# A vision tower with three expert layers: the last layer's blocks write the output, repeated tokens are routed once

## The reference

```python
logits = x @ router_w                       # 8 experts
probs = softmax(logits); p = max(probs); e_idx = argmax(probs)
combine = one_hot(e_idx) * p[:, None]
out = sum over e of combine[:, e] * (relu(x @ wi[e]) @ wo[e])   # 192 -> 768 -> 192
h = _layernorm(h + out)                     # this is the result
```

## Time and profile before

| | us |
|---|---|
| median of 3 runs | 2679.78 |
| lowest and highest run | 2667.89, 2680.46 |
| span of the profiled execution | 2663.7 |
| TensorE busy in it | 2220.1 (83%) |
| VectorE, ScalarE, GpSimd busy | 1463.9, 888.3, 907.3 |

### The profile page before, as it was taken

The page is one execution under the profiler, slowest core; times in us unless marked ns, Lnnn a source line. Parts: engine busy times, 40 slices in busy tenths (PEclk is TensorE's granted clock), DMA queues, the critical chain, the costliest instruction groups (busy, mean ns, idle before and its releaser), DMA issues. The chain is left out here.

```text
span 2663.7 us, 47821 instructions
## 1 busy us (share of the span) xinstructions
PE 2220.1 (83%) x18071; PEld 1965.6 (74%) x18071; DVE 1463.9 (55%) x3517; ACT 888.3 (33%) x1921; POOL 907.3 (34%) x817
## 2 busy tenths in 40 slices
PE   8999995699699749987999889998999967564792
PEld 8888883477588639985766679998999966443692
DVE  2677767566577746227999733332432236866213
ACT  0333336522254313334555411111111114764111
POOL 0323235600100253338776502301111136554325
PEclk9999986699899759998999989999999989555796
DMA  9500000160000336540000050104666631002452
GB/s 271 184 1 1 1 1 19 37 192 2 1 2 2 140 94 184 176 131 21 16 11 6 1 205 26 31 1 160 210 209 211 213 117 39 1 1 79 133 178 74
DMA packets 125725, 225.21 MB, mean 85 GB/s; under 512 B 15862, under 2 KB 96306, under 8 KB 118458
## 3 DMA queue, kind: packets, MB, share of 16 engines
q1 hardware_dynamic: 114938, 203.87, 23.3%
q0 software_dynamic: 10560, 18.29, 2.4%
HBM read 169.06 MB, written 53.02 MB: 83 GB/s over the span
## 5 line engine op out<-in xcount | busy, mean ns | idle before, releaser
L2596 POOL COPY bl_swiglu_w<-ahead_w2swiglu_w 128x1152 f32 x53 | 60.7, 1147 | 370.6 <-PE psum L2648 275.9
L2690 ACT ACTIVATE bl_swiglu_sg<-psum 128x384 f32<-128x384 f32 x106 | 52.0, 490 | 311.9 <-PE psum L2637 311.9
L2626 PE MATMUL psum<-bl_swiglu_xt,bl_swiglu_w 128*128 128x128 f32 x1272 | 152.9, 278 | 1.7 <-DVE bl_swiglu_hid L2727 1.1
L2626 PEld LDWEIGHTS psum<-bl_swiglu_xt,bl_swiglu_w 128*128 128x128 f32 x1272 | 151.0, 194 | 2.3 <-issue 2.3
L2717 DVE COPY bl_swiglu_xt<-psum 128x256 f32<-128x256 f32 x53 | 22.5, 425 | 207.1 <-PE psum L2607 207.1
L2099 POOL DMA_INDIRECT rows_in<-tower_h,tower_spots x66 | 65.3, 990 | 157.2 <-DVE tower_spots L2997 124.3
L2702 ACT ACTIVATE bl_gelu_hid<-psum,bl_gelu_w 128x128 f32<-128x128 f32 x270 | 74.2, 377 | 115.9 <-POOL bl_gelu_w L2596 112.9
L2648 PE MATMUL psum<-bl_swiglu_w,bl_swiglu_hid 128*128 128x192 f32 x636 | 112.1, 327 | 0.0
L2596 POOL COPY bl_gelu_w<-ahead_w2gelu_w 128x1350 f32 x45 | 60.3, 1362 | 149.9 <-DVE bl_gelu_y L2737 136.9
L2929 ACT ACTIVATE shared_sg<-psum 128x432 f32<-128x432 f32 x66 | 35.0, 530 | 206.5 <-PE psum L2866 206.5
L2648 PEld LDWEIGHTS psum<-bl_swiglu_w,bl_swiglu_hid 128*128 128x128 f32 x636 | 102.1, 190 | 0.1
(11 more groups left out here) (683 smaller groups left out, 6062.8 us busy)
## 6 DMA issues: line engine op xcount, KB each, us to landing
bl_swiglu_w<-in_swiglu_w SPq DMA_DIRECT2D x53, 1152.0 KB, 5.2
rows_in<-tower_zeros SPq DMA_DIRECT2D x2, 14592.0 KB, 47.8
bl_gelu_w<-in_gelu_w SPq DMA_DIRECT2D x45, 576.0 KB, 4.0
bl_relu_w<-in_relu_w SPq DMA_DIRECT2D x26, 576.0 KB, 4.1
ahead_w2swiglu_w<-in_swiglu_w SPq DMA_DIRECT2D x1, 9216.0 KB
tok_x<-in_x SPq DMA_DIRECT2D x11, 648.0 KB, 12.5
ahead_w2gelu_w<-in_gelu_w SPq DMA_DIRECT2D x1, 5400.0 KB
bl_swiglu_xr<-rows_in SPq DMA_DIRECT2D x53, 96.0 KB, 2.0
```

The source lines that it names most:

```text
L2596: pool.tensor_copy(w2[:, n % DEEP], w2all[:, e, :].rearrange("p e n -> p (e n)")).then_inc(s_w2, 1)
L2626: pe.matmul(up_tile(n, j, i, side), w[:, o:o + 128], xt[:, n % 2, side, :], start=(i == 0), stop=False, skip_group_check=True)
L2690: act.activation(sg[:, j], bank_pair(n, j)[:, 0, 0:3 * BLOCK].rearrange("p (i n) -> p i n", i=3), ACT.Silu).then_inc(s_silu, 1)
```

## The change

It does these things. (1) Repeated tokens are no longer routed: the tokens are laid so that the last tile begins with image 63 and then repeats 61 and 62, `own` gives the 36 rows of it that are sent, and `chose` is zero for the others. In the gelu and swiglu layers `find_slots` gives the repeated rows the slots of the first ones. `block_count` goes by 2304 rows. (2) In the last layer the row that is sent has two more columns, the gate and the token's row number in the output (`last_rows`, `LAST` = 194), and goes to a DRAM array of its own, `rows_last`, which `clear_last` fills with zeros during the attention stage. (3) A relu block adds its fetched rows to gate times result, takes the variance, and four blocks later scales the rows; GpSimd raises to the power and scatters them to their place in `out` by indirect DMA. Empty rows have token number 0 and go to spare rows ahead of the output. (4) `stage_output` is gone, and so are slots and stores of the last layer. Not shown: `stage_output` as removed, the passing of `cst["xs"]`, the same `choose` and `find_slots` in `stage_shared`, names of tiles and semaphores, and the quantised stage's levelling into the new rows (`rest.level(pool, t, ends[:, t, 0:D])` and the like).

```diff
-MAXB = 53
-DEPTH = (NT * T + BLOCK - 1) // BLOCK
+MAXB = 51
+TOK = 64 * IMG
+DEPTH = (TOK + BLOCK - 1) // BLOCK
 WAY = 4
 FF = 512
+LAST = D + 2
+SPARE = (TOK + (BLOCK - 1) * 8) // BLOCK * BLOCK
...
+def clear_last(sp, cst):
+    sp.dma_start(cst["xl"].rearrange("(a p) n -> p a n", p=128),
+                 cst["fill"][:].unsqueeze(1).broadcast_to([128, 8 * DEPTH + 1, LAST])).then_inc(cst["blank"], 16)
+def last_rows(cst):
+    return cst["xT"][0:T].rearrange("p a n -> p (a n)")[:, 0:NT * LAST].rearrange("p (t n) -> p t n", n=LAST)
...
-    return (NT * T * top + (BLOCK - 1) * E) // BLOCK
+def own(t):
+    return IMG if t == NT - 1 else T
+def choose(dve, chose, iota, picks, a, b, TOP, E):
+    for x, y in ((a, min(b, NT - 1)), (NT - 1, b)):
+        if x < y:
+            rows = own(x)
+            ins = dve.tensor_tensor(chose[0:rows, x:y], iota[0:rows, 0:E].unsqueeze(1).unsqueeze(1).broadcast_to([rows, y - x, TOP, E]),
+                                    picks[0:rows, x:y, :].unsqueeze(3).broadcast_to([rows, y - x, TOP, E]), ALU.is_equal)
+    return ins
+def find_slots(then, dve, cst, sl, found, TOP):
+    then(dve.tensor_tensor(found[:, :, 0:TOP], sl[:], found[:, :, 0:TOP], ALU.add))
+    then(dve.scalar_tensor_tensor(found[:, NT - 1, 0:TOP], found[:, NT - 2, 0:TOP], cst["twice"][:, 0:1], found[:, NT - 1, 0:TOP],
+                                  ALU.mult, ALU.add))
+    then(dve.tensor_copy(cst["slots"][:, 0:TOP].rearrange("p c t -> p t c"), found[:, :, 0:TOP]))
+def send_rows(pool, cst, rows, TOP, tiles, to):
     for t in tiles:
+        n = own(t)
         for c in range(TOP):
-            at = bass.IndirectOffsetOnAxis(ap=cst["spots"][:, t, c:c + 1], axis=0)
-            pool.indirect_dma_start(out=cst["xs"], out_offset=at, in_=rows[:, t, :], in_offset=None).then_inc(cst["sent"], 16)
+            at = bass.IndirectOffsetOnAxis(ap=cst["spots"][0:n, t, c:c + 1], axis=0)
+            pool.indirect_dma_start(out=to, out_offset=at, in_=rows[0:n, t, :], in_offset=None).then_inc(cst["sent"], 16)
             cst["sent_count"] += 16
...
-                    if kind != "swiglu":
-                        if gelu:
-                            pool.wait_ge(cst["clean"], 32)
-                        for g, (a, b) in enumerate(groups):
-                            pool.wait_ge(c_slot, g + 1)
-                            send_rows(pool, cst, rows, TOP, range(a, b))
+                    if gelu:
+                        pool.wait_ge(cst["clean"], 32)
+                    else:
+                        pool.wait_ge(cst["blank"], 16)
+                    for g, (a, b) in enumerate(groups):
+                        pool.wait_ge(c_slot, g + 1)
+                        send_rows(pool, cst, rows, TOP, range(a, b), cst["xs"] if gelu else cst["xl"])
                 @block.tensor
...
                         ins.then_inc(c_T, 1)
-                    act.wait_ge(c_d, 1)
+                        if not gelu and p >= 4 and p % 2 == 0:
+                            powers(act, p // 2 - 2)
                     if gelu:
+                        act.wait_ge(c_d, 1)
                         act.activation(sc[:, 1, :], sc[:, 0, :], ACT.Exp).then_inc(c_e, 1)
                     else:
-                        act.activation(lo[:], lo[:], ACT.Exp).then_inc(c_e, 1)
+                        for g in range((NP - 1) // 2 - 1, NG):
+                            powers(act, g)
                 @block.vector
...
                         a, b = groups[g]
                         n = b - a
+                        if not gelu:
+                            dve.wait_ge(c_e, g + 1)
+                            K.then(dve.tensor_reduce(sc[:, 0, a:b], lo[:, a:b, 0:E], AX, ALU.add))
+                            dve.reciprocal(rows[:, a:b, D], sc[:, 0, a:b])
                         dve.wait_ge(p_m, g + 1)
                         ranked = bank(PO[g % 2])[0:T, 0:n * E].rearrange("p (t e) -> p t e", e=E)
...
                     dve.wait_ge(laid, all_laid)
+                    dve.memset(chose[:, NT - 1], 0.0)
+                    if not gelu:
+                        dve.tensor_copy(rows[:, :, D + 1], cst["token"][:])
                     K.then(dve.tensor_copy(base[:, 0], cst["seed"][:, 0:E]))
...
             @block.sync
             def _(sp):
                 S.arrived(sp, s_w)
+                clear_last(sp, cst)
                 S.clear_before(sp)
...
+        shelves = cst["xl" if last else "xs"].rearrange("(b p) n -> b p n", p=BLOCK)
+        XR = KEPT if last else DEEP
+        WX = LAST if last else D
         w2all = cst["ahead"]["w2" + kind]
         with Stage(nc, "bl_" + kind, cst) as S:
             sg = S.sb("sg", [128, 2, 3, BLOCK])
-            y = S.sb("y", [128, 2, D])
+            y = S.sb("y", [128, KEPT if last else 2, D])
+            to = S.sb("to", [128, KEPT], mybir.dt.uint32)
+            st = S.sb("st", [128, KEPT, 6])
+            mv = S.sb("mv", [128, KEPT, 2])
...
             with nc.Block() as block:
                 @block.sync
                 def _(sp):
                     def fetch_rows(n):
-                        if n >= DEEP:
-                            sp.wait_ge(p_T, n - DEEP + 1)
-                        b = bass.ds(sp.value_load(place[0:1, n:n + 1], min_val=0, max_val=E * DEPTH - 1), 1)
-                        sp.dma_start(xr[:, n % DEEP], shelves[b].rearrange("b p n -> (b p) n")).then_inc(s_x[n % DEEP], 16)
+                        if n >= XR:
+                            sp.wait_ge(c_y if last else p_T, n - XR + 1)
+                        b = bass.ds(sp.value_load(place[0:1, n:n + 1], min_val=0, max_val=E * DEPTH - (not last)), 1)
...
                             store(n - 3)
-                    for n in range(NB if glu else NB - 3, NB):
+                    for n in range(NB if glu or last else NB - 3, NB):
                         store(n)
-                    for x in range(2):
-                        sp.wait_ge(s_st[x], 16 * ((NB + 1 - x) // 2))
+                    ways = len(s_st)
+                    for x in range(ways):
...
                 def _(pool):
+                    def power(n):
+                        x = n % KEPT
+                        pool.wait_ge(c_var, n + 1)
+                        pool.tensor_tensor(rt[:, x:x + 1], vt[:, x:x + 1], cst["half"][:, 0:1], ALU.pow).then_inc(g_root, 1)
+                    def scatter(n):
+                        x = n % KEPT
+                        pool.wait_ge(c_z, n + 1)
+                        pool.indirect_dma_start(out=cst["out"], out_offset=bass.IndirectOffsetOnAxis(ap=to[:, x:x + 1], axis=0),
+                                                in_=y[:, x, :], in_offset=None).then_inc(s_st[x], 16)
                     pool.wait_ge(s_all, 1)
                     for n in range(NB):
                         e = bass.ds(pool.value_load(owner[0:1, n:n + 1], min_val=0, max_val=E - 1), 1)
                         if n >= DEEP:
                             pool.wait_ge(c_y if kind == "gelu" else s_dn, n - DEEP + 1)
                         pool.tensor_copy(w2[:, n % DEEP], w2all[:, e, :].rearrange("p e n -> p (e n)")).then_inc(s_w2, 1)
+                        if last and n >= 4:
+                            power(n - 4)
+                        if last and n >= 6:
+                            scatter(n - 6)
+                    if last:
+                        for n in range(NB - 6, NB):
+                            if n + 2 < NB:
+                                power(n + 2)
+                            scatter(n)
                 @block.tensor
                 def _(pe):
                     def turn(n):
-                        pe.wait_ge(s_x[n % DEEP], arrivals(n))
+                        pe.wait_ge(s_x[n % XR], arrivals(n, XR))
                         if n >= 2:
                             pe.wait_ge(c_T, n - 1 if glu else n - n % 2)
-                        x = xr[:, n % DEEP]
+                        x = xr[:, n % XR]
                         pe.transpose(tp[:, n % 2, 0:BLOCK], x[:, 0:128], ident[:])
                         pe.transpose(tp[:, n % 2, BLOCK:2 * BLOCK], x[:, 64:192], ident[:]).then_inc(p_T, 1)
...
                             dve.wait_ge(s_w2, n + 1)
+                        if last:
+                            x = n % KEPT
+                            if n >= KEPT:
+                                dve.wait_ge(s_st[x], 16 * (n // KEPT))
+                            dve.tensor_tensor(to[:, x:x + 1], xr[:, n % XR, D + 1:D + 2], cst["spare"][:, n:n + 1], ALU.max)
+                            dve.scalar_tensor_tensor(y[:, x], dn[:, n % 2, 0:D], xr[:, n % XR, D:D + 1], xr[:, n % XR, 0:D],
+                                                     ALU.mult, ALU.add).then_inc(c_y, 1)
+                            dve.wait_ge(c_y, n + 1)
+                            K.then(dve.bn_stats(st[:, x, :], y[:, x]))
+                            K.then(dve.bn_aggr(mv[:, x, :], st[:, x, :]))
```

(36 more changed lines are left out.)

125 lines of the change are left out of this document (45 added, 80 removed).

## The result

| | before | after |
|---|---|---|
| median of the runs in one comparison | 2676.70 us (2667.89 to 2680.46, 4 runs) | 2608.73 us (2604.46 to 2612.17, 4 runs) |
| span of the profiled execution | 2663.7 us | 2602.6 us |
| ratio | | 0.9751, 95% interval 0.9730 to 0.9772 |

2614.7 us had been forecast, in a range of 2600 to 2631. The profiled execution has a span of 2602.6 and a time of 2604.46, so 1.9 us lie around the span; in the later runs it was 1.8 to 2.0.

A forecast was written before the change was run, and what follows sets the result against it. TensorE was taken to bound the block stages, GpSimd's chain of gathers the 48.7 us last stretch. Terms -13.1 - 8.7 - 43.6 + 0.7 - 0.4 = -65.1 gave a span of 2598.6, with 16.1 carried 2614.7 us, range 2600 to 2631.

The forecast's parts named there:

- Swiglu blocks: Swiglu layer: block count falls from 53 to 51, two blocks of 6.54 us saved, -13.1 us.
- Gelu pair: Gelu layer: block count falls from 45 to 43, so one whole pair goes, -8.7 us.
- batch statistics: Batch statistics drop two calls shorter than the 0.36 us of a full one, on the path: -0.4 us.
- Relu blocks' steady part: Relu pairs stay 8.72 us; added VectorE work hidden, 2.4 us cover left. T is when a pair of down-products ends.
- The tail: After the last full relu pair ends (T), three scatters follow one another; end at T+13.2, -43.6 us, one block included.
- The relu route: Last layer's routing: gate exponentials and sums move into the loop over six groups, +0.7 us, bounds -0.4 and +3.
- The fill: New 14.4 MB fill at the start of the attention stage is hidden, 0; 48 us if not hidden.
- The time carried: Whole kernel: the median before lies 16.1 us above the profiled span; that distance was added to the forecast span.
- 1 (VectorE the bound): Relu blocks: VectorE operations held for a weight copy's length leave 1.0 us uncovered per pair, 12 us, 2627; chance 0.12.
- 2 (a worse tail): Tail and relu route: late power, slow scatter landings or slips in every group, together +8 us, 2623; chance 0.12.
- 3 (the fill collides): The new fill collides with the loads or the mapping of queues after it: +48 us, 2663; chance 0.02.
- 4 (GpSimd the clock): Relu blocks: GpSimd's queue decides the pair from a scatter of 2.4 us; slower than before, 2692 at 5.5; chance 0.01.

The follow-up runs named there:

- before_again: The kernel before, run once more unchanged: 2671.44 us, one run.
- store_only: The kernel after with the leaving out of repeated tokens undone, so only the last layer's blocks add, normalise and store: 2638.20 us, ratio 0.9852.
- rows_only: The kernel before with only the repeated tokens left out of the three routes, old output stage kept: 2647.90 us, ratio 0.9892.
- the repeats: The kernel before and the kernel after, each run once more unchanged: 2671.44 and 2614.13 us, one run each.
- stats_8: The kernel after with the statistics of each relu block but the last three taken eight times more: 2628.65 us, one run.
- after_timed: The kernel after, unchanged, timed beside other follow-up kernels: 2605.41 us, ratio 0.975.
- pair_late: The kernel after with levellings and scatters one pair behind and the last down-product in a bank of its own: 2607.07 us, ratio 0.9757.
- apart: The kernel after with scatters one pair behind, last down-product in its own bank, and GpSimd's two weight copies behind its two powers: 2608.64 us, ratio 0.9761.
- stats_3: The kernel after with the statistics of each relu block but the last three taken three times more: 2618.55 us, one run.

## Why the prediction was right, and where it was wrong

**Swiglu blocks, -13.1.** Right: first row transposed to last result, 351.4 us in before, before_again and store_only, 338.5 in rows_only and 338.4 in after: -13.0.

**Gelu pair, -8.7; batch statistics, -0.4; slots, 0.** Together with swiglu -22.2 was said; the middle part gives 1539.7 - 1516.6 = -23.1. The gelu blocks alone gave -8.3 (206.2 to 197.9), the quantised stage -0.1 (268.3 to 268.2) where -0.4 was said, and 268.6 and 268.4 in the repeats, so that term is neither shown nor refuted; the rest fell in the gelu route (77.5 to 76.2; 77.7 and 77.0 in the repeats) and between gelu and swiglu blocks (633.0 to 632.2), which were put at 0.

**Relu blocks' steady part, 0.** Right, and for the reason given. The pair after is 8.70. Said was a second sum done at T+2.35; it is at 2590.44, T+2.0. TensorE comes to the next down-products at T+4.6 and not T+4.8, since the 4.81 of the prediction was counted from a rise that begins 0.2 us before the down-products end. So ahead of the second sum 2.6 us are covered and not 2.4. Over the whole pair the cover is wider: VectorE has 2 x 1.50 + 0.67 us of work in 8.70, 5.0 are free, and of the 6.3 us that stats_8 added 1.3 came out as a longer pair (9.98).

**The tail, -43.6.** Said: T at 97.3 us behind the first relu down-product (2606.9 - 2509.64), end at T+13.2. It is 97.2 (2588.44 - 2491.23), and the end is T+14.2. In its steps: sum of 22 at T+0.65, got T+0.5; sum of 23 T+2.35, got T+2.0; last down-product done T+4.5, got T+5.3, as it ran at the lower clock; power of 24 done T+7.9, got T+7.7; last scatter issued T+10.5, got T+10.6. The late last down-product did no harm, as it is not on the path: the last sum waited for the levelling of block 23 (said T+5.9, got T+5.8), as the prediction has it. after_timed shows the same from the other side. Its last down-product took 2.19 us after the same pause, and its end is at T+14.3 all the same:

```profile
2590.04 2.19 PE L2684 MATMUL psum<-bl_relu_w,bl_relu_hid 128*128 128x192 f32 x12 [2.16 <-DVE bl_relu_y L2775]
```

The term that was mis-sized comes last. Said were 2.7 us from the last scatter's issue to the end, taken from a gather's landing; they are 3.6, and 3.6, 3.7 and 3.7 in store_only, pair_late and apart. It isn't the landing that was too short, for the scatters of the kernel after landed (min/median/max over all 25):

```profile
DMA to landing us min/median/max: 2.3/2.4/5.1
```

By the trace SyncE, which waits for the last scatter, goes on at 2601.35, 2.3 us after its issue. GpSimd's draining instruction at the end of the stage ends at 2602.40, and the span at 2602.63. So 1.3 us of closing the stage behind the last landing were put at nothing. In the kernel before, the stores at the end are SyncE's, GpSimd's drain is over at 2661.89, and the span ends 0.4 us after SyncE goes on (2663.28).

**The relu route, +0.7.** From its first tile to the first row transposed it took 47.9 and 48.2 us before, 49.0 and 49.1 after, 49.3 in store_only, 47.8 in rows_only: +0.9 to +1.1, inside the bounds, and it belongs to the half of the change that store_only has. The way is as said: the first scatter begins 12.4 us behind the route's start (10.0 before), the later ones then follow without the pauses of before, the last ends at 40.6 (39.6 before), and what follows up to the first row is as long as it was (8.3 to 8.5). One table load, as said (L2287, 1283 ns).

**The fill, 0.** Right; 48 us was its price without cover, 45.1 were measured.

**Not foreseen.** The first relu down-product came 1.1 later behind the first row than in the first profile: the first rise took 5.41 us at a granted clock of 0.54 (4.46 before). In before_again it took 5.46, so this too differs between runs of one kernel. The sum was -65.1; against the two profiles of before, middle and last part together gave -63.8 and -65.9. Profile against profile it was -61.1, of which +2.7 is the first part.

**The time carried, 16.1 us, was wrong.** The forecast added to the span the distance from the profiled span to the median of before. Only 1.9 us lie around a span; the other 14 were one fast execution against slower ones. After's median is 6.1 above its profiled span. So 6.0 us too much was forecast: 10.0 too much carried, less 4.0 by which the gain was overrated. That the two errors had opposite signs is luck; the span alone was forecast 4.0 too low.

**The rivals.** 1 (VectorE the bound): refuted by stats_3, but its mechanism exists. The profile after has one levelling of 1.51 us, from 2584.86, beside a weight copy from 2585.09 to 2586.25; it lay under cover. The Trainium skill (SBUF — State Buffer, "SBUF: two separate sides") says that VectorE and GpSimd share a pair of ports as an exclusive lock, which concerns VectorE's two-port operations and those with two inputs in SBUF. The trace agrees: the levelling (SBUF to SBUF) and the row number (two inputs in SBUF) were held, and the sum, one input of which lies in PSUM, was never over 0.42 us. Of the same section's warning, that a GpSimd-issued DMA waits for such an operation, little shows: a scatter issued while a levelling had 0.2 us to go (2596.31) took 1.13 us, the next 0.96. The 6775 ns row is of the same kind: it runs from 1389.58 to 1396.35 beside five operations of GpSimd in a row, the last of which ends at 1396.13. 2 (a worse tail): +8 was said, +1.0 came. 3 (the fill collides): refuted for where the fill stands. 4 (GpSimd the clock): with twice the scatters the pair was still 8.7.

## What to carry to other kernels

A stage that only gathers, normalises and stores can go under TensorE's time, if each engine's added work per turn is summed against the turn, and what is left at the end is counted in the queue of the slowest issuer: a scatter that lags six blocks behind leaves six to do alone. Place GpSimd's long copies in VectorE's pauses, or small VectorE operations from SBUF to SBUF grow to the copy's length; here that shortened the last part, while a gain in the whole time was not shown. For a forecast of some us, carry only what lies around a span (here 1.9 us) and compare stages that the change touches; the first part, which but for the fill is the same in all of these kernels, moved by 16 us between runs.

## What the runs showed of the hardware that was not expected

- A weight copy of GpSimd of 1.15 us stretched a levelling from 0.37 to 1.50 us and two of them in a row a one-column operation from 0.16 to 2.04, until the end of the second.
- The last scatter's issue lies 3.6 to 3.7 us before the end of the span, though it landed after 2.3: GpSimd's drain at the end of the stage is over 1.05 us after SyncE goes on.
- After a pause of 2.15 us the last down-product took 3.11 us at a granted clock of 0.79; after the same pause it took 2.19 in after_timed, at 1.00.
- One fill of 14065 KB landed after 62.6 us in the attention stage and 59.1 in the relu route, where 13824 KB of rows two columns narrower took 45.6: 27 to 35% more per byte. The trace has one packet for each row, of 776 and of 768 bytes. The Trainium skill (DMA: Bandwidth & Descriptors, "How a descriptor splits into AXI transactions") says that a descriptor is cut at multiples of 256 bytes, the rest and a start between them costing extra. A row was 768 bytes and is 776 now. By that rule it would be slower, and the trace agrees in sign, but no run here changed the width alone.
